# Cross-attention with explicit V against a folded value-output matrix, in a gated attention and FFN layer on one core

## What is computed

```python
# cross-attention, B=32, 56 queries, 16 heads of 64, D=128
q = (layernorm(x) @ Wq);  k = (ctx @ Wk);  v = (ctx @ Wv)     # each split into 16 heads of 64
scores = einsum('bhqd,bhkd->bhqk', q, k) / sqrt(64), masked to k <= q
attn = softmax(scores);  out = einsum('bhqk,bhkd->bhqd', attn, v)
x = x + tanh(g_xattn) * (out.reshape(b, 56, 1024) @ Wo)
# FFN block on layernorm(x): per token, 16 heads attend to 16 heads (head size 8),
# then a softmax gate over 8 experts, each a 128x128 matrix
x = x + tanh(g_ffn) * ffn(layernorm(x))
```

## Time and profile before

| | |
|---|---|
| median of the runs | 283.18 us |
| the profiled execution, whole | 282.62 us |
| its span, first to last instruction | 280.7 us |
| PE busy | 248.0 us (88%), 2350 matmul instructions |
| DVE busy | 209.7 us (75%) |
| ACT, POOL busy | 159.8 us (57%), 153.5 us (55%) |

### The profile page before, as it was taken

The page is one execution under the profiler, slowest core; times in us unless marked ns, Lnnn a source line. Parts: engine busy times, 40 slices in busy tenths (PEclk is TensorE's granted clock), DMA queues, the critical chain, the costliest instruction groups (busy, mean ns, idle before and its releaser), DMA issues.

```text
span 280.7 us, 6097 instructions
## 1 busy us (share of the span) xinstructions
PE 248.0 (88%) x2350; PEld 184.3 (66%) x2350; DVE 209.7 (75%) x370; ACT 159.8 (57%) x432; POOL 153.5 (55%) x189
## 2 busy tenths in 40 slices
PE   7989899998999999999999999999999796852660
PEld 6776589685969695959595959585968374621220
DVE  0266623599989898989897429999998979998500
ACT  2536424554686858576767575657677364633431
POOL 4104032335468585758585554545859476759444
PEclk9999999999999999999999999999999799996665
DMA  6995000000000000000000000000000000000000
GB/s 213 352 349 227 0 4 0 2 1 2 2 0 12 0 13 0 13 1 12 0 12 2 9 2 9 4 2 1 11 0 2 11 2 9 1 9 0 12 9 9
DMA packets 7483, 9.28 MB, mean 33 GB/s; under 512 B 542, under 2 KB 5919, under 8 KB 7327
## 3 DMA queue, kind: packets, MB, share of 16 engines
q1 hardware_dynamic: 7022, 8.25, 9.0%
q10 hardware_dynamic: 432, 0.64, 0.6%
HBM read 7.97 MB, written 0.92 MB: 32 GB/s over the span
## 4 chain that ended last, share of the span: by engine, by line
PE 73%; DVE 8%; POOL 7%; ACT 6%; issue 5%; POOLq 0%; ACTq 0%; DVEq 0%
PE ps_a L681 37%; PE ps_b L681 13%; PE ps_c L681 11%; PE ps_b L723 4%; PE ps_e L681 4%; POOL exb L294 2%; ACT zT L372 2%; DVE prod L560 1%; DVE ps_e L546 1%; PE ps_b L678 1%; POOL probs L265 1%; ACT exb L427 1%; ACT probsT L386 1%; POOL exb L296 1%; DVE prod L537 1%
## 5 line engine op out<-in xcount | busy, mean ns | idle before, releaser
L681 PE MATMUL ps_a<-zT,m_sb 128*128 128x112 f32 x512 | 62.5, 276 | 1.6 <-ACT zT L372 1.1
L681 PEld LDWEIGHTS ps_a<-zT,m_sb 128*128 128x128 f32 x512 | 60.1, 192 | 3.1 <-ACT zT L372 1.3
L265 POOL TENSOR_TENSOR probs<-probs,prinv 120x672 f32<-120x672 f32 x16 | 24.3, 1517 | 41.5 <-DVE prinv L510 41.5
L274 POOL TENSOR_TENSOR prod<-fqkv 128x768 f32<-128x768 f32 x14 | 25.4, 1816 | 23.4 <-DVE fqkv L532 23.4
L427 ACT ACTIVATE exb<-ps_c,gate 128x128 f32<-128x128 f32 x112 | 32.3, 383 | 7.0 <-PE ps_c L681 5.5
L681 PE MATMUL ps_c<-fwe_sb,x2T 128*128 128x512 f32 x56 | 31.9, 699 | 4.9 <-DVE glog L587 4.9
L379 ACT ACTIVATE probs<-ps_b,rstd 120x896 f32<-120x896 f32 x15 | 15.1, 1007 | 34.0 <-PE ps_b L681 34.0
L546 DVE TENSOR_REDUCE ps_e<-prod 128x256 f32<-128x2048 f32 x14 | 32.0, 2285 | 0.1
L571 DVE TENSOR_REDUCE oraw<-prod 128x128 f32<-128x2048 f32 x14 | 31.2, 2227 | 0.0
L537 DVE TENSOR_TENSOR prod<-ps_e,fqkv 128x1280 f32<-128x1280 f32 x14 | 20.9, 1492 | 11.2 <-ACT ps_e L398 11.2
L294 POOL TENSOR_TENSOR exb<-exb 128x640 f32<-128x640 f32 x14 | 21.6, 1539 | 13.1 <-ACT exb L427 13.0
(11 more groups left out here) (124 smaller groups left out, 448.7 us busy)
## 6 DMA issues: line engine op xcount, KB each, us to landing
ctx_sb<-in_ctx SPq DMA_DIRECT2D x1, 1024.0 KB, 10.4
xp_sb<-in_xp SPq DMA_DIRECT2D x1, 896.0 KB, 9.6
out<-out_sb SPq DMA_DIRECT2D x14, 64.0 KB, 1.5
xT<-in_x_t SPq DMA_DIRECT2D x1, 784.0 KB, 6.2
cT<-in_ctx_t SPq DMA_DIRECT2D x1, 784.0 KB, 8.2
wvt_sb<-in_wv_t SPq DMA_DIRECT2D x1, 512.0 KB, 7.8
wo_sb<-in_wo SPq DMA_DIRECT2D x1, 512.0 KB, 9.0
ctx_sb<-in_ctx SPq DMA_DIRECT2D x2, 256.0 KB, 9.8
```

What stands on the lines that cost most here:

```text
L265: nc.gpsimd.tensor_tensor(pr[0:TG, NC:C, :, 0:S], pr[0:TG, NC:C, :, 0:S], prinv[p % 2][0:TG, NC:C, :].unsqueeze(3).to_broadcast([TG, C - N ...
L274: nc.gpsimd.tensor_tensor(prod1[:, 0:HP, :, :], t[:, D:2 * D].rearrange("p (g d) -> p g d", g=FH).unsqueeze(1).to_broadcast([128, HP, FH, ...
L681: return nc.tensor.matmul(o, lhsT, rhs, start=start, stop=stop, skip_group_check=True)
```

## The change

V is made after all: `values(p, bt)` multiplies the transposed context of one batch (128x64, stationary) by the weights of all heads of row group r (128x512, moving), once for r = 0 into partitions 0 to 63 and once for r = 1 into partitions 64 to 127 of one bank of ps_a. ACT copies it to `v_sb`. It is done for the next pair at the end of a step. `attend(p)` is 32 matmuls of 56x64 by 56x56 on the four quarters of the array, in the order row group and column group (0,0), (1,1), (1,0), (0,1), where the first two go to one bank of ps_a and the last two to the other. ACT copies the result to `aT`, two heads on top of each other, so that `new_y` needs 8 matmuls with Wo (`wo_sb`, whose halves of chunks 4 to 7 are swapped) instead of 16. `combine`, `m_sb` and the loads of the natural context (2 MB) go. The mask is now set by four 64x64 matmuls. The second bank pair in which `mix` worked, ps_b, is no longer needed for it: `scores(t)` waits only for the copies of the transposed probabilities.

The order changes on all engines: `new_y` stands whole right behind `scores`; on DVE `new_x1` and the probability sums go ahead of the tile's small work, `scaled_qkv` ahead of `mixed_heads`; on POOL `second_scale` goes behind `norm`, `residual` to the start; on ACT the projections' copies go ahead of `squares`, both expert copies to the end. HP becomes 8 and HQ 5 (more of the products on POOL).

```diff
-HP = 6
-HQ = 3
+HP = 8
+HQ = 5
... (DVE, in the loop over t)
                 if t < NP:
                     score_max(t)
+                if t <= NP:
+                    new_x1(t - 1)
                 if fb is not None:
                     logits(fb)
+                if t < NP:
+                    prob_sums(t)
+                    norm(t)
...
 (POOL, in the loop over t)
                 if t < NP:
                     norm(t)
+                if fc is not None:
+                    second_scale(fc)
...
 (PE)
+            def values(p, bt):
+                b, n, ys = USES["v", p, bt]
+                free_bank(b, n, ys)
+                t0 = (2 * p + bt) * S
+                for r in range(2):
+                    ins = mm(ps_a[r * G:(r + 1) * G, b, :], cT[:, t0:t0 + G], wv_sb[:, r, :])
+                ins.then_inc(a_full[b], 1)
...
-                for r in range(2):
-                    if p >= 2:
-                        pe.wait_ge(z_free[r], p)
+                if p >= 2:
+                    last = p if p > 2 else 1
+                    pe.wait_ge(s["pT_lo"], last)
+                    pe.wait_ge(s["pT_hi"], last)
+                for bt, r in ((0, 0), (1, 1), (1, 0), (0, 1)):
                     rows = slice(r * G, r * G + S)
-                    mm(banks[0:TG, r, 0:C * S], both_b[rows, :, :].rearrange("p b q -> p (b q)")[:, 0:TG],
+                    mm(banks[bt * G:(bt + 1) * G, r, 0:C * S], ident_b[rows, r * G:(r + 1) * G],
                        hide_b[rows, :, :].rearrange("p c k -> p (c k)"), stop=False)
...
+            def attend(p):
+                pe.wait_ge(s["pT_lo"], p + 1)
+                pe.wait_ge(s["pT_hi"], p + 1)
+                for half in range(2):
+                    b, n, ys = USES["o", p, half]
+                    free_bank(b, n, ys)
+                probs_t, v = probsT[p % 2], v_sb[p % 2]
+                for ch in range(4):
+                    for bt in range(2):
+                        for half, r in ((0, 0), (0, 1), (1, 1), (1, 0)):
+                            c, j = 4 * half + ch, half ^ r
+                            ins = mm(ps_a[j * G:(j + 1) * G, USES["o", p, half][0], ch * T + bt * S:ch * T + (bt + 1) * S],
+                                     v[r * G:r * G + S, bt, c, :], probs_t[r * G:r * G + S, c, bt * S:(bt + 1) * S])
+                            if ch == 3 and bt == 1 and r == (0 if half else 1):
+                                ins.then_inc(a_full[USES["o", p, half][0]], 1)
...
+            def new_y(p):
+                for b in range(2):
+                    pe.wait_ge(a_free[b], USES["y", p][b])
+                if p:
+                    pe.wait_ge(s["x1T_ready"], p)
+                for ch in range(C):
+                    ins = mm(ps_a[:, 0, 0:T], wo_sb[:, ch, :], aT[p % 2][:, ch, :], start=(ch == 0), stop=(ch == C - 1))
+                ins.then_inc(s["y_made"], 1)
...
 (PE, in the loop over t)
                     scores(t)
+                if t <= NP:
+                    new_y(t - 1)
                 if fc is not None:
                     turn_o(fc)
...
                     expert_half(fc, 0)
+                if t < NP:
+                    attend(t)
+                if fc is not None:
                     expert_half(fc, 1)
-                if t < NP:
-                    mix(t, 1)
-                    mix(t, 0)
+                if t + 1 < NP:
+                    values(t + 1, 0)
+                    values(t + 1, 1)
```

More of the change, by code:

```diff
@@ L58, in fill, with fills, build @@
         uses[name] = (b, count[b], ys[0] if b == 0 else 0)
-    def projections(kind, g, which=range(4)):
+    def fills(kind, g, which):
         for k in which:
             fill((kind, g, k), 1 - k % 2)
-    def mixes(p):
-        for r in range(2):
[L66 to L80, removed]
+    def new_y(p):
+        uses["y", p] = tuple(count)
+        ys[0] += 1
+    fills("k", 0, range(4))
+    fills("q", 0, range(4))
+    fills("v", 0, range(2))
+    fills("q", 1, range(4))
+    fills("v", 1, range(2))
+    fills("k", 1, range(4))
+    fills("o", 0, range(2))
+    new_y(0)
+    fills("o", 1, range(2))
+    fills("v", 2, range(2))
+    for t in range(2, NP + 1):
+        new_y(t - 1)
         for kind, g, k in PROJECT_AT.get(t, ()):
-            projections(kind, g, (k,))
+            fills(kind, g, (k,))
         if t < NP:
-            mixes(t)
+            fills("o", t, range(2))
+        if t + 1 < NP:
+            fills("v", t + 1, range(2))
     return uses
 USES = bank_uses()
-def build(nc, xp, x_t, ctx2, ctx_t, wq, wk, wv_t, wo, fw, fup, fdn, fwe, out):
+def build(nc, xp, x_t, ctx_t, wq, wk, wv, wo, fw, fup, fdn, fwe, out):
     with ExitStack() as stack:
@@ L248, in _ @@
             pool.wait_ge(s["consts"], 6)
[L249 to L253, removed]
+            nc.gpsimd.tensor_copy(ident_b[:, :], ident[:, :]).then_inc(s["consts"], 1)
+            pool.wait_ge(s["consts"], 7)
             nc.gpsimd.tensor_copy(hide_b[:, :, :], hide[:, :].unsqueeze(1).to_broadcast([128, C, S])).then_inc(s["mask_ready"], 1)
@@ L436, in _ @@
                 project("q", 0, k)
+            values(0, 0)
+            values(0, 1)
             exps(0)
@@ L653, in _ @@
                     shifted_logits(fb)
-                if t <= NP:
-                    new_x1(t - 1)
-                if t < NP:
-                    prob_sums(t)
-                    norm(t)
-                if fb is not None:
-                    weighted(fb)
                 if fc is not None:
@@ L805, in _ @@
             scores(1)
-            pe.wait_ge(s["wvt_in"], 16)
-            pe.wait_ge(s["wo_in"], 16)
-            combine(0)
+            pe.wait_ge(s["wv_in"], 16)
+            values(0, 0)
+            values(0, 1)
             shift(0)
@@ L889 @@
     xp[:, :S] = x.reshape(NP, 2, S, D).transpose(1, 2, 0, 3)
-    ctx2 = np.zeros((2, G, 2 * NP, D), np.float32)
-    ctx2[:, :S] = ctx.transpose(1, 0, 2)
+    ctx_t = np.zeros((D, NP * T + G - S), np.float32)
+    ctx_t[:, :NP * T] = ctx.reshape(-1, D).T
+    wo = i["L0_xattn_Wo"].reshape(C, 2, DK, D).copy()
+    wo[C // 2:] = wo[C // 2:, ::-1]
     col = lambda a: a.reshape(-1, 1)
```

196 lines of the change are left out of this document (75 added, 121 removed).

## The result

The changed kernel takes **297.52 us** (median of 4 runs, 297.2 to 297.72); the kernel before, beside it, 283.10. The ratio is 1.0509 [1.0485, 1.0533]: slower by 5%, where no change was forecast; the time still lies in the range of 272 to 299. The profiled execution took 297.72 us, its span is 295.6, so 14.9 us are to be found.

The account below looks back on a forecast made before the run. PE was full, with DVE 0.7 us behind; after the change a ring through all engines would hold 14.42 us a step. Terms -0.4, +0.9, +0.4, -0.2, 0, -0.8 sum to -0.1: 283.0 us, range 272 to 299.

Parts of the forecast that it names:

- R1: Rival on PE: `attend`'s row groups collide in a bank and its matmuls go in pairs; +16, 299 us; chance 0.15.
- PE's added and removed work: PE per step: 4.26 us removed, 3.23 added (masks, `attend`, `values`), so its work falls from 14.49 to 13.46.
- R2: Rival on PE: column groups of `values` run one after the other, +1.82 us a step; 308 us; chance 0.1.
- R3: Rival: rings are looser, PE stays full and a step is its work, 13.46 us; 272 us; chance 0.15.
- The first ring: Once around all engines per step, from scores through y, logits, sums, normalisation, experts, `attend`, `values`, masks: 14.42 us.
- DVE's own ring: DVE's work per step after savings, plus a 0.88 us wait for r2 before the gate logits: 14.3 us.
- Step 11: Step without experts: nothing covers ACT's copies, waits of 0.75 and about 0.7; 14.05 against 13.19 us, +0.9.
- Steps 2 to 4: Early steps, some without experts or logits: 13.0 + 14.05 + 14.42 = 41.5 against 41.12 us, +0.4.
- Steps 12 to 14 and the tail: Late steps 3 x -0.07 = -0.2 us; tail -0.8 from less DVE work, less POOL's late weighted share.
- Head: Start of the kernel: PE's lost and gained work within 0.5 us of each other, taken as 0.

Follow-up runs that it names:

- e10: e3 with `ve` made by ACT instead of DVE; 288.07 us, ratio 1.0171.
- e3: Changed kernel with `onorm`'s input, the last reduction's result, placed in PSUM, same order and shares; 290.26 us (282.81 to 290.59).
- e1: Changed kernel with POOL's products ahead of `residual` again; 290.3 us (285.69 to 290.59).
- e6: e3 with `tile_stats` (and so `ve`) ahead of `gate_logits` on DVE and `x1_copy` ahead of `head_exps` on ACT; 300.24 us, ratio 1.0602.
- e4: e3 with `ve` as a tensor_scalar, one tensor input and a scalar per partition; 288.16 us, ratio 1.0137.
- e2: Changed kernel with POOL's shares of before (HP 6, HQ 3); 290.0 and 290.18 us in two runs, 295.15 and 295.44 in two.
- e9: e3 with idle matmuls on PE where it waits in steps 2, 3, 11, 14 and 15; 290.65 us, ratio 1.026.
- e12: e10 with the idle matmuls of e9; 289.56 us, ratio 1.0239.

## Why the prediction was wrong, point by point

That 297.52 us lies in the range of 272 to 299 is luck: the range reached so far up for R1, a slow `attend`, and that did not happen.

- **PE's added and removed work: right.** Masks 0.22 (0.33 taken), `attend` 1.08 (1.08), `values` 1.87 (1.82). R1 said `attend` would take 2.16, R2 `values` 3.64; both are refuted. The rule on which R1 leaned does not hold for this pattern: "TensorEngine Tiling (Array Packing)" of the Trainium skill, Restrictions and Gotchas, Gotcha 1, keeps different row tiles out of one PSUM bank. Here two row groups that write different halves of the partitions of one bank take 1.08 us for 64 instructions, next to 0.93 for `scores` with a bank each. The measurement decides; it doesn't show what the same partitions would do. R3 fell with e10: with no held row a step is 14.65, not 13.46. In e3's step of 14.70 only 0.39 is a wait that the rows name, so PE's work with the turns between its groups is 14.3, above the 13.46 of the forecast: the two expert halves take 2.01 start to start now that `attend` stands between them (1.82 before), the projection 3.30 (3.17 before); the rest is in smaller pieces that were not taken apart.
- **The first ring: right in kind, 0.28 too short.** 14.42 was taken, e3 shows 14.70. The terms that were too small are the experts (1.82, measured 2.01), the transposes' wait (1.67, 1.78) and y (1.97, 2.07). It costs nothing in the changed kernel's full steps, where DVE's ring is longer, but without the held `onorm` (e3) steps 5 to 10 still take 87.99 us, 1.5 more than the forecast of 6 x 14.42.
- **DVE's own ring: the step that failed.** It reads "less a fifth of the products (0.30) and 2/13 of the weighted ones (0.29)" and "`normed_heads` directly behind the reduction that it reads adds about 0.1". Both savings came (products 1492 to 1214 ns, weighted 1877 to 1605). But every other DVE row was carried over at its duration before, though there `onorm` had begun ahead of POOL's row and `ve` had none over it; what comes to lie under what in the new order was not weighed. `onorm` costs 1.1 us more and `ve` 0.4, and 14.3 + 1.5 = 15.8 against 15.69 measured. In steps 5 to 9 this is the +6.0. e1 and e3 take away the first of the two, by order and by place, and the step falls by 1.0 each time, to where the first ring holds. The Trainium skill has the rule, in "SBUF — State Buffer", Who interferes with whom: a DVE instruction with two inputs in SBUF and a GpSimd instruction that reads SBUF share a port pair, and the later one is blocked for the whole of the other. The traces agree on the rows of that form: 1.39 and 0.55 us ending with POOL's row, 0.29 with one input in PSUM, 1.39 for two elements in e6. The form with one tensor input, held in e4, is not covered by this sentence of it. By that rule, applied to the new order, a step would have come out near 15.8, as an estimate up to 13 x (15.8 - 14.42) = 18 us more than forecast; it was not weighed.
- **Step 11: +0.9 taken, +2.9 measured.** The waits of 0.75 and 0.7 were named (measured 0.69 and 0.59). That the clock can fall behind them was not, and it is the other 2.0: in e1, e2 and e6 the same step runs at a clock of 1.00 and takes 14.10, against the 14.05 forecast, and in e9, with idle matmuls in the gaps, 14.28.
- **Steps 2 to 4: +0.4 taken, +1.3 measured, and not by the clock,** which is 1.00 there. They take 13.09, 14.18 and 14.76 where 13.0, 14.05 and 14.42 were forecast, 0.6 more together. The rest is in the base: the chain's row at 81.30 is not the start of step 5, whose masks stand at 80.87, so these steps took 40.76 before and not 41.12.
- **Steps 12 to 14 and the tail: -0.2 and -0.8 taken, +4.1 and +0.6 measured.** e1, without the held `onorm`, has 45.65 us in steps 12 to 14, 3.7 less and only 0.4 above before. One held `onorm` lies in step 13 (15.82 us, 14.65 in e1), two lie in step 14 (18.08, 16.17); step 12 has none and is longer by 0.6, since the low clock of step 11 lasts into its scores (1.65 us instead of 1.00). In step 14 the lower clock takes part too (0.81, 0.89 in e1), so the two causes are not separated there. In the tail e1 has the same clock, 0.66, and takes 54.09: about 1.0 of the 1.4 missed goes with the held `onorm`. The rest was not taken apart; e9 and e12 only show that filling PE there does harm.
- **Head: right**, 40.08 against 40.11.

What stays open: why the same waits are followed by the lower clock in some executions and steps and not in others (step 3 against step 11 of the changed kernel), whether that alone makes the two groups of times in e1 to e3, and which wait starts each fall after step 14.

## What to carry to other kernels

When an edit moves work on DVE or POOL, list which DVE instructions with two inputs in SBUF, or of another form seen held (e4), fall under which POOL instruction in the new order, and price each at the rest of that POOL row, not at its duration before; even one of two elements can pay for nearly the whole POOL row (161 ns became 1390 in e6). A place in PSUM for one input or an order that lets POOL finish first took it away for `onorm` (1071 ns to 291 and 292), ACT as the engine for `ve` (532 ns to 294). And where two rings stand within tenths of a microsecond of each other, as here, a saving in one is worth only that distance.

## What the runs showed of the hardware

- The form with one tensor and a scalar per partition is held like the one with two tensors (547 against 540 ns), even for two elements a partition. ACT's row of 0.29 us wholly under POOL's in e10 is not.
- A plain copy from SBUF to SBUF is held too. One stands in the head of both kernels; in the changed one it begins 0.26 us behind POOL's normalisation and ends 0.08 behind its end (DVE's group before and its row after; POOL after):

```profile
L617 DVE COPY bdb<-fup_sb 65x128 f32<-65x128 f32 x1 | 0.2, 214 | 0.0
...
23.67 1.34 DVE L605 COPY bdb<-fup_sb 65x128 f32<-65x128 f32 x1
...
23.41 1.52 POOL L254 TENSOR_TENSOR probs<-probs,prinv 120x672 f32<-120x672 f32 x1 [0.20 <-DVE prinv L504]
```

- A held instruction has no wait in the trace: its row is longer and ends with POOL's.
- Waits of 1.14, 0.69 and 0.59 us with work between them, in a stretch where PE had been nearly full, were followed by the lower clock in step 11 of the changed kernel (3.68 instead of 1.94 us for `values`). The same waits left it at 1.00 in step 3 of that kernel and in step 11 of e1, so they are not enough by themselves. Single waits of up to 0.96 us a step in steps 5 to 9 left it at 1.00.
